# Writing a loop over 52 pairs of images out as straight-line code, in a kernel of one core

## What is computed

```python
h = concat([token, patches(x) @ W.T + b], 1) + pos      # (128, 197, 128)
h = concat([h, txt], 1)                                 # (128, 325, 128)

# attention by phases, on n = ln(h)
key, query = exp(1j*pi*tanh(n @ Wk + bk)), exp(1j*pi*tanh(n @ Wq + bq))   # 4 sets of 8 planes
V = n @ Wv + bv
total = sum_s weights[s] * real(sum_planes(cumsum(key_s * V) * conj(query_s)))
gate = sigmoid(n @ Wg + bg)
total = gate * total + (1 - gate) * position_part(V)
h = h + n + (total / norm) @ Wo + bo

# 64 experts, 2 for each token, at most 256 tokens each, on n = ln(h)
scores, experts = top_2(sigmoid(n @ gate_w.T))
shared = silu(n @ sw1) * (n @ sw3) @ sw2
routed = sum over the 2 experts: score * (silu(n @ w1[e]) * (n @ w3[e]) @ w2[e])
return h + shared + routed
```

## Time and profile before

| | us |
|---|---|
| median of 3 runs | 1777.86 |
| lowest, highest | 1775.88, 1781.35 |
| the profiled execution | 1779.21 |
| its span in the trace | 1777.4 |
| TensorE clock granted, mean of the span | 0.958 |

### The profile page before, as it was taken

The page is one execution under the profiler, slowest core; times in us unless marked ns, Lnnn a source line. Parts: engine busy times, 40 slices in busy tenths (PEclk is TensorE's granted clock), DMA queues, the critical chain, the costliest instruction groups (busy, mean ns, idle before and its releaser), DMA issues. The chain is left out here.

```text
span 1777.4 us, 36202 instructions
## 1 busy us (share of the span) xinstructions
PE 1572.3 (88%) x9606; PEld 1161.5 (65%) x9606; DVE 1512.8 (85%) x6004; ACT 1103.0 (62%) x1869; POOL 1229.1 (69%) x1162
## 2 busy tenths in 40 slices
PE   2799999999999999999999999999999982576662
PEld 1577777777777777777777777777777761455551
DVE  2589999999999999999999999999999983687661
ACT  2777777777777777777777777777777631111110
POOL 0117777777777777777777777777777777588888
PEclk9899999999999999999999999999999995898885
DMA  9867676666666666666666666666666201466653
GB/s 168 222 162 141 137 135 129 126 124 120 116 113 112 110 109 108 108 106 107 105 108 105 108 105 107 105 105 106 105 108 108 57 17 33 95 113 98 94 81 34
DMA packets 259896, 193.28 MB, mean 109 GB/s; under 512 B 65513, under 2 KB 239268, under 8 KB 259656
## 3 DMA queue, kind: packets, MB, share of 16 engines
q1 hardware_dynamic: 206008, 173.72, 53.1%
q0 software_dynamic: 51200, 17.87, 8.4%
q10 hardware_dynamic: 2576, 0.60, 0.4%
HBM read 84.84 MB, written 83.73 MB: 95 GB/s over the span
## 5 line engine op out<-in xcount | busy, mean ns | idle before, releaser
L564 POOL DMA_INDIRECT slot_rows<-xs,slot x768 | 825.4, 1075 | 219.4 <-issue 211.6
L557 POOL TENSOR_TENSOR rs<-ve,neg_half 128x6 f32<-128x6 f32 x128 | 172.2, 1345 | 258.0 <-DVE ve L1227 258.0
L623 ACT ACTIVATE img<-img 84x980 f32<-84x980 f32 (+1 forms) x192 | 341.9, 1782 | 0.6 <-DMA img<-img 0.6
L840 PE MATMUL bank<-img,w_tok 126*128 126x392 f32 (+1 forms) x640 | 224.3, 497 | 11.3 <-DMA img<-img 11.3
L604 POOL DMA_INDIRECT out_rows<-img,etok x128 | 199.9, 1562 | 29.7 <-issue 29.0
L676 ACT ACTIVATE xs<-h,nb,rs 128x128 f32<-128x128 f32 x384 | 154.7, 482 | 34.1 <-DVE nb L1287 34.1
L840 PEld LDWEIGHTS bank<-img,w_tok 126*128 126x128 f32 (+1 forms) x640 | 118.1, 192 | 84.4 <-issue 14.1
L921 PE MATMUL bank<-a_t,v 128*128 128x325 f32 (+2 forms) x768 | 167.0, 353 | 1.1 <-DVE a_t L1281 1.1
L903 PE MATMUL bank<-pos_a,v 128*128 128x325 f32 (+2 forms) x768 | 167.6, 354 | 0.0
L692 ACT ACTIVATE xh<-h,nb,rs 128x128 f32<-128x128 f32 x384 | 154.0, 482 | 3.6 <-DVE nb L1287 3.6
L921 PEld LDWEIGHTS bank<-a_t,v 128*128 128x128 f32 (+1 forms) x768 | 130.1, 190 | 27.8 <-issue 1.4
(11 more groups left out here) (192 smaller groups left out, 3677.7 us busy)
## 6 DMA issues: line engine op xcount, KB each, us to landing
img<-in_x SPq DMA_DIRECT2D x384, 150.1 KB
img<-img SPq DMA_DIRECT2D x256, 160.8 KB
img<-img SPq DMA_DIRECT2D x128, 128.6 KB
out_rows<-fin SPq DMA_DIRECT2D x128, 128.0 KB
slot_rows<-xs,slot POOLq DMA_INDIRECT x768
slot_rows<-init_rows SPq DMA_DIRECT2D x16, 540.0 KB, 5.3
img<-slot_rows SPq DMA_DIRECT2D x32, 270.0 KB
h<-in_txt SPq DMA_DIRECT2D x64, 128.0 KB, 2.5
```

The costliest lines, as they stand in the source:

```text
L557: g.tensor_tensor(out=rs[:, q.u], in0=ve[:, q.u], in1=neg_half[:, :], op=ALU.pow).then_inc(s_rs, 1)
L564: g.indirect_dma_start(out=slots_d, out_offset=bass.IndirectOffsetOnAxis(ap=slot[0:nt, q.x, r, part:part + 1], axis=0), in_=xs[0:nt, q.x, ...
L623: a.activation(cols[:, b0:b0 + nb, :], raw[:, q.u, :].rearrange("p (t b) -> p b t", b=P)[:, b0:b0 + nb, :], ACT.Copy)\
L840: ins = mm(bank[:, 4, 0:2 * PATCHES], w_tok[r, m, :], xk[r, k.u, :, m, :], start=(m == 0), stop=(m == SHIFT - 1))
```

## The change

`steps` no longer makes a loop. All pairs from the first to the last are written out, with numbers in place of registers, on all five engines. Nothing else is edited; the loop over the experts stays as it is.

```diff
 def steps(eng, body, begin=0):
 
-    for k in range(begin, HEAD):
-        body(Pair(None, None, k))
-    turns = (TAIL0 - HEAD) // 4
-    assert HEAD + 4 * turns == TAIL0 and HEAD % 4 == 0
-    with eng.Fori(HEAD // 4, HEAD // 4 + turns) as j:
-        four = j * 4
-        for c in range(4):
-            body(Pair(four, j, c))
-    for k in range(TAIL0, PAIRS + SKEW + 1):
+    for k in range(begin, PAIRS + SKEW + 1):
         body(Pair(None, None, k))
```

## The result

| | before | changed |
|---|---|---|
| median of 5 runs, us | 1777.86 | 1767.93 |
| lowest, highest | 1775.88, 1781.35 | 1763.96, 1769.53 |
| ratio, 95% interval | | 0.9943 [0.9931, 0.9956] |
| span of the profiled execution | 1777.4 | 1762.7 |

The changed kernel is 9.9 us faster by the medians (1767 was predicted, with a range from 1762 to 1772.5). The page of the changed kernel answers to the earlier trace rows: busy times by engine, the slices of PE and its clock; then come the two queues that bring instructions (packets, MB, share).

A forecast was written before the change was run, and what follows sets the result against it. PE was taken to bound each pair at 21.76 us, DVE 0.9 us behind. 1779.2 - 11.1 (DVE's branch) + 0 + 0 = 1768.1 us; from the median 1766.8, said as 1767, range 1762 to 1772.5.

The forecast's parts named there:

- The branch on DVE: In the loop over pairs, 12 taken branches halt DVE, 0.92 us each on the mean; removing them gains 11.1 us.
- the 55 steps: Sign: from DVE's first instruction of pair 8 to that of pair 63, 1196.6 us expected instead of 1207.70.
- Registers and addresses: Register arithmetic for waits and SP's addresses in the loop lies under PE's and DVE's work; removing it gives 0.
- PE's straight-line code: 48 more written-out pairs make PE fetch 55 more instruction packets of 16 KB, hidden, so cost 0.
- The bound from above: Most that one new PE instruction packet could cost: 0.92 us, as DVE's halt; 0 was taken.
- never stops except at a taken branch: DVE fetches instructions all the time in the loop and halts only at taken branches; no cost for straight-line DVE code.
- the steps of 22 us or more: Sign of being wrong: pair steps this long at regular places would mean late instructions.
- That the halt is a fetch: DVE's 2.8 us behind its branch read as fetching the loop's beginning again, from one 8 KB packet.
- Behind the pairs: Last scatters and expert stage move forward by 11.1 us, expert stage as long as before, 1 us allowed either way.
- near 1503.2: Sign: start of the last scatter in us, expected 11.1 us before the earlier 1514.33.
- Pairs did not settle at 21.96 us: Rival: SP's transfers or POOL need 21.96 us a pair, so time stays at 1777.9 us; chance 0.08.
- PE didn't stop in straight-line code: Rival: PE stops for late instruction packets, 0.92 us each, 51 us in all, giving 1818 us; chance 0.05.

The follow-up runs named there:

- dve_8: The kernel before with DVE's loop at eight pairs a turn, the other engines at four: 1770.15 us, ratio 0.9965.
- dve_only: The kernel before with DVE alone written out, the other engines keeping the loop of four pairs a turn: 1767.33 us, ratio 0.9943.
- all_but_dve: The kernel before with PE, ACT, POOL and SP written out, DVE alone keeping its loop: 1776.74 us, ratio 0.9997.
- pe_8: The kernel before with all engines but PE written out, PE's loop at eight pairs a turn: second run 1774.88 us, ratio 0.9990.

## Why the prediction was right

*The branch on DVE*, 11.1 us: right in mechanism and place, and within a tenth in size. Removed, the 55 steps are 10.03 us shorter; the long steps of the kernel before add up to 12 x 0.92 = 11.0 us, and `dve_8` has the price for five of them at 1201.38 us. `dve_only` and `all_but_dve` show that it is DVE's alone.

*Registers and addresses*, 0: right, `all_but_dve`.

*PE's straight-line code*, 0: right. 55 packets more were expected and 52 came, and no step is long for them. The bound from above, DVE's halt, was real in another place: `pe_8` pays 1.64 us where PE takes a branch out of what it keeps.

*DVE "never stops except at a taken branch"*: slightly wrong. Written out, four of its borders cost 0.35, 0.27, 0.11 and 0.07 us, 0.8 us in all. This is the term that I had at zero, and most of what the steps came short of 11.1 by. Two of them, 22.11 and 22.03 us, are the steps of 22 us or more that I had named as a sign of late instructions; they cost 0.6 us together.

*That the halt is a fetch*: argued from one packet then. Now the size of the turn switches it on and off on PE and ACT, and DVE halts at 390 rows a turn and not at 154.

*Behind the pairs*, unchanged within 1 us: right for the experts, 243.1 to 242.4. I had not counted the drain, where the clock moves the last scatter by 3.4 us from one execution to the next. For that reason, and for a start that was 1.6 us earlier, the last scatter began at 1499.37 us and not near 1503.2, and the profiled executions differ by 14.7 us, the medians by 9.9.

*The rivals.* Pairs did not settle at 21.96 us: no other engine had used the 0.92 us. PE didn't stop in straight-line code.

## What to carry to other kernels

Compare the pair (or tile) that holds a loop's back edge with its neighbours; if it is longer, look at each sequencer's next instruction behind the branch, and at the length of the branch itself. Only the engine whose turn is longer than what it keeps pays (here 390 rows on DVE, 566 on ACT and 2260 on PE, but not 154, 192 and 1130), and it was enough to write out that one engine, or to make its turns longer and fewer. Put the back edge where the engine has work queued, where few DMAs run and where nobody waits for the first instruction of the next turn; the wrong place cost this kernel 42 us.

## What the hardware showed that I had not expected

A taken branch that must fetch costs a sequencer 2.5 to 3.4 us at DVE and ACT, and 3.3 to 3.9 us at PE, where it stands as the duration of the branch. With the DMA engines 88% busy it was up to 5.3 us on DVE. Straight-line fetching isn't quite free: up to 0.35 us at a few of the places where a block of 128 of DVE's instructions begins. And a loop that doesn't fit draws more instruction packets than the same work written out: 60 against 36 on queue 14.
